# Decoder layer, attention stage: the sums' matmuls moved to stand directly behind a key block's value matmuls, a third PSUM bank for the transposed scores, row maxima turned on VectorE and placed by DMA, reciprocals on a compact tile

## The reference

```python
q = _heads(x @ Wq, B, L, nh, hd)                     # B=2, L=2048, nh=16, hd=32
k_s, v_s = ...(x @ Wkv_short)                        # attention a=0 ("short")
k_l, v_l = ...(x @ Wkv_long)                         # attention a=1 ("long")
decay_bias = -|pos_q - pos_k| * (1 - decay_factor)
out_short = softmax(q @ k_s.T / sqrt(hd) + decay_bias) @ v_s
out_long  = softmax(q @ k_l.T / sqrt(hd)) @ v_l
out = alpha * out_short + (1 - alpha) * out_long     # alpha = sigmoid(mix_weight)
return out @ Wo
```

## Time and profile before

| what | value |
|---|---|
| median of 3 runs | 5613.65 us (5612.13 to 5614.03) |
| the profiled execution, first to last instruction | 5613.5 us |
| attention, first score matmul to the last `sums` matmul | 641 us to 4273 us of it |
| busy share over the span: PE, DVE, ACT, POOL | 96%, 74%, 51%, 52% |
| mean granted TensorE clock | 0.981 of full speed |

### The profile page before, as it was taken

The page is one execution under the profiler, slowest core; times in us unless marked ns, Lnnn a source line. Parts: engine busy times, 40 slices in busy tenths (PEclk is TensorE's granted clock), DMA queues, the critical chain, the costliest instruction groups (busy, mean ns, idle before and its releaser), DMA issues. The chain is left out here.

```text
span 5613.5 us, 97704 instructions
## 1 busy us (share of the span) xinstructions
PE 5382.8 (96%) x28780; PEld 2121.9 (38%) x28780; DVE 4180.9 (74%) x7218; ACT 2874.8 (51%) x5201; POOL 2933.2 (52%) x658
## 2 busy tenths in 40 slices
PE   7999899999999999999999999999996999999999
PEld 3444333333322323223233332232332555555555
DVE  5444688877877878778778787787883777777777
ACT  1111166666666666666666666666664333333332
POOL 0000088878877878778778787788884000000000
PEclk9999799999999999999999999999998999999999
DMA  4333201010101010101010101010101000000000
GB/s 135 105 104 93 81 19 33 21 29 22 33 21 29 21 34 21 29 21 33 22 29 21 34 21 29 21 33 22 29 3 49 17 22 17 22 17 22 17 22 12
DMA packets 145632, 191.62 MB, mean 34 GB/s; under 512 B 18500, under 2 KB 97988, under 8 KB 145030
## 3 DMA queue, kind: packets, MB, share of 16 engines
q1 hardware_dynamic: 145159, 185.65, 11.2%
HBM read 123.56 MB, written 61.64 MB: 33 GB/s over the span
## 5 line engine op out<-in xcount | busy, mean ns | idle before, releaser
L764 DVE TENSOR_REDUCE rowmax_parts<-scores_qk 128x1 f32<-128x512 f32 x4096 | 2569.8, 682 | 668.9 <-PE scores_qk L836 666.3
L745 ACT ACTIVATE probs_T<-scores_kq 128x512 f32<-128x512 f32 x4096 | 2263.3, 596 | 1249.5 <-PE scores_kq L836 1195.2
L704 POOL TENSOR_TENSOR probs_group_sum<-probs_T 128x2048 f32<-128x2048 f32 x384 | 1742.4, 4538 | 667.4 <-PE sums L913 395.7
L836 PE MATMUL scores_kq<-q_operand,k_operand 103*128 103x512 f16 (+3 forms) x3712 | 1279.8, 351 | 16.7 <-ACT probs_T L745 15.4
L704 POOL TENSOR_TENSOR probs_group_sum<-probs_group_sum,probs_T 128x2048 f32<-128x2048 f32 x256 | 1185.5, 4631 | 46.0 <-POOL probs_group_sum L704 45.1
L836 PE MATMUL scores_qk<-k_operand,q_operand 96*128 96x512 f16 (+4 forms) x3712 | 1178.9, 354 | 22.8 <-DMA k_operand<-positions_dram 18.5
L903 PE MATMUL outputs_T<-probs_T,v_operand 128*32 128x512 f32 x8192 | 1103.3, 611 | 52.4 <-issue 52.4
L836 PEld LDWEIGHTS scores_qk<-k_operand,q_operand 96*128 96x128 f16 (+1 forms) x3712 | 352.7, 98 | 898.6 <-DVE rowmax_parts L764 627.1
L1341 PE MATMUL f_gate_up<-w_gate_up,xq_T 128*128 128x352 f32 x2048 | 626.4, 462 | 0.8 <-issue 0.8
L836 PEld LDWEIGHTS scores_kq<-q_operand,k_operand 103*128 103x128 f16 x3712 | 361.2, 98 | 672.9 <-ACT probs_T L745 507.1
L1341 PEld LDWEIGHTS f_gate_up<-w_gate_up,xq_T 128*128 128x128 f32 x2048 | 382.5, 190 | 200.7 <-issue 2.6
(11 more groups left out here) (144 smaller groups left out, 3477.2 us busy)
## 6 DMA issues: line engine op xcount, KB each, us to landing
qk_parts_dram<-qk_parts SPq DMA_DIRECT2D x96, 256.0 KB, 2.5
q_operand<-qk_parts_dram SPq DMA_DIRECT2D x192, 128.0 KB, 2.6
k_operand<-qk_parts_dram SPq DMA_DIRECT2D x192, 128.0 KB, 2.9
v_dram<-v_heads SPq DMA_DIRECT2D x16, 1024.0 KB, 5.4
v_operand<-v_dram SPq DMA_DIRECT2D x64, 256.0 KB, 3.1
q_operand_above<-qk_parts_dram SPq DMA_DIRECT2D x96, 128.0 KB, 2.8
x_groups<-x SPq DMA_DIRECT2D x8, 1024.0 KB, 8.8
attention_dram<-o_mixed SPq DMA_DIRECT2D x128, 64.0 KB, 1.6
```

The lines of the kernel that those rows point to most:

```text
L704: nc.gpsimd.tensor_tensor(total, first, probs[:, b % PBUF, :], ALU.add).then_inc(added.sem, 1)
L745: nc.scalar.activation(probs[:, kb % PBUF, qt * BANK:(qt + 1) * BANK], pb[:, k % 2, :], ACT.Exp)\
L764: nc.vector.reduce_max(rowmax[:, w % 2, c // NQ, c % NQ:c % NQ + 1], pa[:, k % 3, :], AX.X)\
L836: return nc.tensor.matmul(out, lhsT, rhs, start=start, stop=stop, skip_group_check=True)
```

## The change

Five things change, all in `attend`.

1. **Order on PE.** A step is now `times_v(j)`, then directly behind it any `count` that is due (steps `COUNT_AT` = 4, 7, 10, 13, 15 and 17, one step earlier than before; 17 is step 1 of the next unit), then four pairs of one transposed and one plain score matmul. The transposed scores run `LEAD` = 7 chunks ahead of the values (six before), the maxima 20 chunks further than one unit (`EARLY`; 16 before).
2. **Banks.** `scores_kq` has three banks. The third is the bank that `turned` had.
3. **Maxima.** `turn_max` on PE and `round_max` on ACT go. DVE writes the negated maxima as fp16 into the first 16 of 32 columns of `negmax` and transposes it itself in 32x32 blocks into `negmax_T` (128x32). The row of 2048 maxima then lies in four groups of partitions, so `place_max` copies it with four DMAs per operand, in pieces of 32 fp16 values, where it was one.
4. **Reciprocals.** `sums` holds each denominator 32 times over (32 equal partitions per quarter). Four DMAs now gather one partition of each quarter into `sums_compact` (128x16), one `reciprocal` inverts that, one DMA writes it to a scratch in DRAM, and four DMAs read it back, each broadcast to 32 partitions of `sums_inverse`.
5. **Order on DVE, ACT and SP.** `invert` stands before the 13th maximum of a unit, `weigh` before the 29th, `mix` before the 33rd, `take` before the 61st; `take_sums` before key block 3 of ACT (block 4 before). SP does, for each unit: gather, spread, store (every second unit), `place_max`, then the loads of the next pass.

The diff, cut to its core (the printed functions above show the old side):

```diff
-ASTEPS = 12
-TURN_MAX = 12
-INVERT = 3
-WEIGH = 8
-MIX = 10
+BURST = 1
+STEPS = KB // BURST
+SLOTS = BURST * NQ
+LEAD = SLOTS + 3
+EARLY = 20
+TAKE_SUMS = 3
+INVERT = 12
+WEIGH = 28
+MIX = 32
+TAKE = (STEPS - 1) * SLOTS
-COUNT_LAG = 3
+COUNT_AT = (4, 7, 10, 13, 15, 17)
...
-        negmax = sb("negmax", [P, 2, KB], F32)
-        maxT = sb("negmax_T", [KB, 2, P], F16)
+        negmax = sb("negmax", [P, 2, HD], F16)
+        maxT = sb("negmax_T", [P, 2, HD], F16)
+        sums_c = sb("sums_compact", [P, KB], F32)
+        inv_c = sb("inverse_compact", [P, KB], F32)
...
-        pb = ps("scores_kq", [P, 2, BANK], F32)
+        pb = ps("scores_kq", [P, 3, BANK], F32)
-        pt = ps("turned", [P, BANK], F32)
...
             def place_max(w, n):
-                sp.wait_ge(roundm.sem, roundm.at(n, w + 1))
+                sp.wait_ge(turned.sem, turned.at(n, w + 1))
                 for dst in (q_op[w], q_up[w]) if w % 2 == 0 else (q_op[w],):
-                    sp.dma_start(dst[MROW:MROW + 1, :], maxT[:, w % 2, :]).then_inc(maxrow[w].sem, 16)
+                    row = dst[MROW:MROW + 1, :].rearrange("o (c g j) -> o c g j", g=NQ, j=HD)
+                    for g in range(NQ):
+                        sp.dma_start(row[:, :, g, :], maxT[g * HD:g * HD + KB, w % 2, :]).then_inc(maxrow[w].sem, 16)
+            def gather_sums(w, n):
+                wait_apart(sp, sums_out, sums_out.at(n, w + 1), passed)
+                wait_apart(sp, inverted, inverted.at(n, w), passed)
+                for qt in range(NQ):
+                    sp.dma_start(sums_c[qt * HD:(qt + 1) * HD, :], sums[qt * HD:qt * HD + 1, :].rearrange("o (r e) -> o r e", e=KB))\
+                        .then_inc(gathered.sem, 16)
+            def spread_inverse(w, n):
+                wait_apart(sp, inverted, inverted.at(n, w + 1), passed)
+                sp.dma_start(inv_scr[w % 2:w % 2 + 1, :].rearrange("o (p e) -> (o p) e", e=KB), inv_c[:, :])\
+                    .then_inc(inv_out.sem, 16)
+                wait_apart(sp, inv_out, inv_out.at(n, w + 1), passed)
+                wait_apart(sp, weighed, weighed.at(n, w), passed)
+                for qt in range(NQ):
+                    sp.dma_start(inv[qt * HD:(qt + 1) * HD, :],
+                                 inv_scr[w % 2:w % 2 + 1, qt * BANK:(qt + 1) * BANK].to_broadcast([HD, BANK]))\
+                        .then_inc(inv_in.sem, 16)
...
                 for w in range(UNITS):
+                    back = unit_before(w, n, first)
+                    if back:
+                        gather_sums(*back)
+                        spread_inverse(*back)
+                        if back[0] % 2:
+                            store(back[0] // 2, back[1])
                     if after(w, n, last):
                         place_max(*after(w, n, last))
-                    if w == 0 and not first:
-                        store(1, n - 1)
-                    if w == 2:
-                        store(0, n)
...
             def negate(w, n):
-                nc.vector.tensor_reduce(negmax[:, w % 2, :], rowmax[:, w % 2, :, :], AX.X, ALU.max, negate=True)\
+                nc.vector.tensor_reduce(negmax[:, w % 2, 0:KB], rowmax[:, w % 2, :, :], AX.X, ALU.max, negate=True)\
                     .then_inc(maxed.sem, 1)
+                dve.wait_ge(maxed.sem, maxed.at(n, (w + 1) * (CHUNKS + 1)))
...
+                nc.vector.transpose(maxT[:, w % 2, :], negmax[:, w % 2, :]).then_inc(turned.sem, 1)
...
-            def invert(w, n, r):
-                dve.wait_ge(sums_out.sem, sums_out.at(n, w + 1))
-                nc.vector.reciprocal(inv[:, r * P:(r + 1) * P], sums[:, r * P:(r + 1) * P]).then_inc(inverted.sem, 1)
+            def invert(w, n):
+                dve.wait_ge(gathered.sem, gathered.at(n, (w + 1) * NQ))
+                dve.wait_ge(inv_out.sem, inv_out.at(n, w))
+                nc.vector.reciprocal(inv_c[:, :], sums_c[:, :]).then_inc(inverted.sem, 1)
             def weigh(w, n):
                 dve.wait_ge(taken.sem, taken.at(n, w + 1))
-                dve.wait_ge(inverted.sem, inverted.at(n, (w + 1) * NQ))
+                dve.wait_ge(inv_in.sem, inv_in.at(n, (w + 1) * NQ))
...
+                    for j in range(STEPS):
+                        for kb in range(BURST * j, BURST * (j + 1)):
+                            times_v(w, n, kb)
+                        for u, behind in (((w, n), 0), (back, STEPS)):
+                            for g in range(GROUPS_N):
+                                if u and COUNT_AT[g] == j + behind:
+                                    count(*u, g)
+                        for s in range(SLOTS):
+                            b = j * SLOTS + s + LEAD
+                            if b < CHUNKS:
+                                scores_for_exp(w, n, b)
+                            elif ahead:
+                                scores_for_exp(*ahead, b - CHUNKS)
+                            distance, c = maximum_of(j * SLOTS + s)
+                            unit = after(w, n, last, distance)
                             if unit:
-                                scores_for_max(*unit, chunks[c])
+                                scores_for_max(*unit, c)
```

More of the change, by code:

```diff
@@ L529, in adds_until, with maximum_of, last_with @@
     return sum(max(0, sum(b <= max(kb, g[1]) for b in g) - 1) for g in GROUPS if g[0] <= kb)
-def chunks_of(i):
-    k = (i - ASTEPS) % KB * NQ
-    return (1 if i < ASTEPS else 2), list(range(k, k + NQ))
-EARLY = (KB - ASTEPS) * NQ
+def maximum_of(g):
+    c = (g + EARLY) % CHUNKS
+    return (1 if g + EARLY < CHUNKS else 2), c
+def last_with(k, ring, total):
+    return max(m for m in range(total) if m % ring == k)
 ROW_LOADS = UNITS + 6 * UNITS // 2
@@ L581, in attend @@
         opened = [Rises(sem(f"a_opened{w}"), 10 - 3 * (w % 2), 16) for w in range(UNITS)]
[L582 removed]
+        maxrow = [Rises(sem(f"a_maxrow{w}"), (2 - w % 2) * NQ, 16) for w in range(UNITS)]
         scoredA = Rises(sem("a_scored_qk"), UNITS * CHUNKS)
@@ L731, in one_pass @@
                     for kb in range(KB):
-                        if back and kb == COUNT_LAG + 1:
+                        if back and kb == TAKE_SUMS:
                             take_sums(*back)
-                        if kb == (TURN_MAX + 2) % KB and after(w, n, last):
-                            round_max(*after(w, n, last))
                         old = w * KB + kb - PBUF
@@ L802, in one_pass @@
                 for w in range(UNITS):
-                    ahead, back = after(w, n, last), unit_before(w, n, first)
-                    for i in range(KB):
-                        if i == KB - 1:
+                    back = unit_before(w, n, first)
+                    for g in range(CHUNKS):
+                        if g == TAKE:
                             take(w, n)
-                        if back and INVERT <= i < INVERT + NQ:
-                            invert(*back, i - INVERT)
-                        if back and i == WEIGH:
+                        if back and g == INVERT:
+                            invert(*back)
+                        if back and g == WEIGH:
                             weigh(*back)
-                        distance, chunks = chunks_of(i)
+                        if back and g == MIX and back[0] % 2:
+                            mix(back[0] // 2, back[1])
+                        distance, c = maximum_of(g)
                         unit = after(w, n, last, distance)
-                        for c in chunks if unit else ():
+                        if unit:
                             max_chunk(*unit, c)
@@ L816, in one_pass @@
                                 negate(*unit)
-                        if back and i == MIX and back[0] % 2:
-                            mix(back[0] // 2, back[1])
             one_pass(0, True, False)
@@ L824, in _ @@
             end = (UNITS - 1, PASSES - 1)
-            for r in range(NQ):
-                invert(*end, r)
+            invert(*end)
             weigh(*end)
@@ L853, in scores_for_max @@
                     pe.wait_ge(opened[w].sem, opened[w].at(n, opened[w].per_pass))
-                pe.wait_ge(maxed.sem, maxed.at(n, k - 2 + (k - 3) // CHUNKS if k >= 3 else 0))
+                if k >= 3:
+                    pe.wait_ge(maxed.sem, maxed.at(n, k - 2 + (k - 3) // CHUNKS))
+                else:
+                    m = last_with(k, 3, UNITS * CHUNKS)
+                    pe.wait_ge(maxed.sem, maxed.before(n, m + 1 + m // CHUNKS))
                 bank = pa[:, k % 3, :]
```

89 lines of the change are left out of this document (30 added, 59 removed).

## The result

The changed kernel takes 5711.93 us (median of 4 runs, 5709.91 to 5715.11), the kernel before 5613.42 us (4 runs, 5612.13 to 5614.03): the ratio is 1.0177, 95% interval 1.0162 to 1.0191. It is 1.8% slower, and I had forecast 2.1% faster. The profiled execution has a span of 5710.4 us.

A forecast was written before the change was run, and what follows sets the result against it. PE was taken to bound the kernel, at 108.82 us a pair of units. With 31 pairs saving 121 us, the last units 5 and the tail adding 6, 5613.5 - 121 - 5 + 6 = 5494 us; range 5460 to 5550.

The forecast's parts named there:

- The count behind the values: PE's count directly behind the values adds 0.88 us against 1.09: 0.21 saved, twelve times, 2.5 us a pair.
- Three banks and one order: PE's scores: alternating kinds and a third bank leave 0.15 us margin; the third transposed score's wait goes, within 1.6 us.
- the sum: PE's time for a pair of units: 91.2 + 2.9 + 12 x 0.88 + 0.2 = 104.9 us, 3.9 less.
- Maxima, Reciprocals: Two steps: PE loses two transposes a pair, DVE 4 x 0.94 us a unit; the gather lands with 1.1 us margin.
- the 6 forecast: Kernel's tail: 3.4 us of reciprocals replaced by gather, small reciprocal and DMAs out and in, +6 us.
- The rival of a late gather: DVE, and PE with it, stands still every unit waiting for the gather: slower, 5660 us; chance 0.05.
- POOL: POOL's adds: a group of three takes at most 9.6 us, three steps 9.7; counts covered by 1.9 us.
- What mix and weigh still cost: DVE's mix, 0.7 us in a bare step, can delay the maxima: 0.2 us a pair added.
- The loop's back edges stay: PE's 3.97 us wait and slower clock at the loop's edge: 7.8 us, fourteen times, untouched by the change.

The follow-up runs named there:

- e6_count_mid: e1_gap with the denominators' matmuls moved from directly behind the values to the middle of the step, three banks kept; 5609.01 us.
- e4_merge_only: The kernel before with only the count moved from the middle of the step to directly behind the values; 5617.58 us, ratio 1.0004.
- e1_gap: The changed kernel with the weighing moved before a unit's 57th maximum and the mix behind its last, where GpSimd is idle; 5525.53 us.
- e10_act_edge: e1_gap with ScalarE's loop turned by one key block, so its branch comes four exponentials later, beside TensorE's; 5503.94 us.
- e9_four_slots: e1_gap with the weighing ahead of maximum 25, 27, 29 or 30, one place for each unit of a pass; 5658.07 us.

## Why the prediction was wrong

- **The count behind the values.** Right: in the changed kernel the sums start 0.88 us behind the values in the median, and 0.21 was forecast for each, 0.24 measured by e6_count_mid's pair. Its condition, the third bank and the new order, I had put in a step of its own worth 1.6 us a pair; that is what e6_count_mid has over the kernel before, 107.17 for 108.82. e4_merge_only shows that the merge is worth next to nothing without them.
- **Three banks and one order.** Right: steps of 2.85 to 3.03 and 3.70 to 3.89 us, and without the waits for POOL's adds a pair of 104.28 where the sum had 104.9: 19 us better over 31 pairs. What it missed is the place where the ring of three banks doesn't close, 0.65 us in each of 15 passes, 10 us.
- **Maxima, Reciprocals.** Right: VectorE waits for the gather 5 times in 64, 19.8 us in all, of which 10.9 and 8.3 stand in the last unit and the tail, where no maximum is behind it, and the tail is 5.2 us longer for the 6 forecast. The rival of a late gather did not happen, though the kernel is slower.
- **POOL.** Right in what it says: the adds hold up no count in the loop. What the adds hold up otherwise it doesn't ask.
- **What mix and weigh still cost.** This is the step that failed. I counted the mix at its 0.7 us and the weighing at nothing, and never asked what runs on POOL when they start: an instruction of VectorE with two SBUF inputs is held until POOL's add ends. POOL is busy 45.7 of 54 us, so where I didn't know their place relative to an add, the bounds were 0 and 4.5 us for each, and the range had to hold them. A sign stood in my own rows: POOL's add of 4.82 beside 4.54 us. It stands behind a weighing that was served first, as the one of 4.78 in the timeline above; the 546 adds of the kernel before that don't start beside a weighing or a mix take 4.51 to 4.55. Measured: 5.1 us a pair, plus 1.6 us a pass of lower clock. Taken over 15.5 passes that is 183 us; e1_gap gives 186.
- **The loop's back edges stay.** The second failure. I took PE's wait and the slower clock as the edge, and held that nothing here touches it. An edge cost 11.1 us for 8.0, 40 us over 13 edges (I had counted 14). In the mean of the 13, PE's wait for ACT went from 0.76 to 1.64 us, its own wait ahead of the first value block from 4.03 to 3.54, a second wait inside that block from 0.18 to 1.21, and the stretch at the lower clock behind it is 10.2 against mostly 6.8 us long. e10_act_edge takes away the wait for ACT by moving ACT's branch, and gets 21.6 us back. Why ACT and PE each stop a second time in the changed kernel, no run shows; that part stays open.

Summed again with these terms: 5494 + 183 + 40 - 19 + 10 = 5708 us, for 5710 of the profiled span and 5712 measured.

## What to carry to other kernels

Where GpSimd works through long SBUF operations, a VectorE instruction with two SBUF inputs can cost the time left of the one under way; read the duration's median and maximum for the same instruction (0.77 and 4.55 us here), and place it in a gap or give it one input. Look at each engine's own loop branch: where one engine needs results from behind another's branch before it reaches its own, the two stand in a row, and turning one loop by a block took 1.66 us off an edge here. When a ring of buffers doesn't divide the uses of a pass, look for a wait where it closes. Try a change of order together with the buffers that it needs, since either alone can show nothing or a loss.

## What I had not expected of the hardware

- The wait for POOL's add is for all of it, even when VectorE comes 0.05 us behind its start (5.03 us). The Trainium skill (SBUF — State Buffer, Who interferes with whom) says of VectorE's two-port modes that whoever issues first has the shared pair for the whole instruction. Here an instruction with two SBUF inputs behaves so. And whoever is second is late in both directions: an add that starts while a weighing runs takes 4.73 to 4.84 us for 4.54, in the kernels before and after and in e9_four_slots.
- Behind two waits of 1.3 and 1.8 us, five us apart from start to start, TensorE's granted clock fell to its lower level for 3.4 us, in 13 of 15 first units; the value block behind them takes 1.73 us, not 1.06. Behind the same two waits in the third units it fell in 3 of 16. What makes the difference isn't shown. In e9_four_slots such a fall took the price of one wait from 3.3 to as much as 6.1 us.
- A branch costs an engine more than one wait. In the changed kernel ACT is held up twice (2.31 and 2.20 us, the first put down to PE by the profile), PE 3.19 and then 1.29 us inside its first value block.
